# Finishing of output blocks moved and split differently, and the first visit's masks reordered, in a one-core masked graph attention

## The chip, the cores and the metric

The kernel runs on one core of one Trainium2 chip. The metric is the device time of one execution in microseconds (us), lower is better. Five engines work side by side, each through its own instructions in order: TensorE (PE; PEld are its weight loads), VectorE (DVE), ScalarE (ACT), GpSimd (POOL) and the sync engine (SP), which here only issues transfers. They wait for each other by counting semaphores.

## What is computed

```python
h = maximum(layernorm(x), 0)                      # x is 8192 x 256, float32
e = leaky_relu(h @ a[:256] + (h @ a[256:]).T, 0.01)   # 8192 x 8192
att = softmax(where(adj > 0, e, -9e15), axis=1)   # adj is 8192 x 8192, int32
out = x + att @ h
```

A row of adj without any edge gets the mean of h as its result (the softmax of equal values). The kernel calls this the row's share of the mean.

## The kernel before

**Weights.** The exponential of the leaky relu splits into factors of the row and of the column, so a tile of weights is `max(r, g) * mask`, with r laid out along the rows of a block (`r_rep`), g one number per column, and q, the third factor, folded into h. VectorE makes it (`weights`, L766), from the mask turned so that columns lie on partitions (`T8`). For float32 accuracy the weights are split into a rounded part `w_hi`, which ScalarE makes (`round_w`, L534 and L537), and the rest `w_lo`, which VectorE makes (`subtract`, L777 and L781). h times q is split in the same way into `h_hi` (ScalarE) and `h_lo` (GpSimd: `scale_h` L372, `rest_h` L389, L391). TensorE adds three products per tile: hi by hi, lo by hi, hi by lo (`row_tile`, L929 to L932).

**Blocks and visits.** The output has 16 row blocks of 512 rows; columns come in 16 chunks of 512. A chunk is two pairs of 128-column tiles; a pair is 24 products on TensorE. A visit keeps one block's sums in PSUM (`acc`) over some chunks. The first 24 visits do a quarter of the columns (4 chunks, 8 pairs) each; their sums are kept in DRAM (`part_sums`). Then come 8 turns of `finals(m)`, each with a *short visit* (block m, the last quarter, 8 pairs) and a *long visit* (block m+8, all 16 chunks, 32 pairs).

**The mask.** Per chunk ScalarE turns adj into a mask (`convert`, L524, 2 us). Until about 600 us TensorE turns it (L896); in the last visits VectorE does (L747, once per chunk).

**Slots.** Every engine walks through the pairs with the same `steps`. Extra work is hung on slot k of a visit by `side_work(V, k)`: k is 0 to 3 in a visit's first step, 4 to 7 in its second, and 8 to 11 in the last step of a long visit. In slot k VectorE makes `w_lo` of pair k-2, then side work, then the weights of pair k. TensorE may start pair k when `w_hi` and `w_lo` of pair k are there; `w_lo` has two buffers, so VectorE is at most two pairs ahead.

**Finishing.** A block that is complete is finished during the next visit. ScalarE copies the sums out of PSUM into `stage` (`evacuate`, slot 1). In a long visit the block is one whose first three quarters lie in DRAM: ScalarE issues the load of them (`load_prior`, slot 0) and GpSimd adds them (`add_prior`, L400, four instructions). VectorE then makes the reciprocal row sums and the flags of empty rows (`denominators`, L794 to L800, slot 3 in a short visit and slot 4 in a long one). For each of four row tiles ScalarE scales the sums (L591) and makes the share of the mean (`hshare`, L592), and GpSimd adds both to x in `xb` (`finish`, L409 and L411). There is one `hshare`, so ScalarE waits for GpSimd's last add before it goes on:

```python
act.wait_ge(s_o, i)      # in normalise(f, t)
```

x of the block is loaded again in slot 2 (`load_x_again`), and the result is stored from the ScalarE queue in slot 7 of a short and slot 8 of a long visit (`store_out`).

**The first visit** (`head`) makes h for chunks 0 to 3 while it uses it. For each chunk VectorE also makes the scores of the next one (`scores`, L734, eight instructions with their reads) and layer norm statistics (`stats`, L708, L714). TensorE turns the mask of the next chunk behind a chunk's first (even) pair.

## Time and profile before

| what | value |
|---|---|
| time, median of 3 runs | 1568.66 us (1568.29 to 1571.74) |
| the profiled execution: its own time | 1571.44 us |
| its span, first to last instruction | 1569.7 us |
| busy: TensorE, VectorE, ScalarE, GpSimd | 1526.8, 1498.5, 1187.6, 384.0 us |
| mean granted TensorE clock | 0.998 |

The profiled execution took 1.74 us more than its span and lies 2.78 us above the median of the three runs. Busy time is a count of the time in which an engine ran an instruction; it says nothing of who waited for whom, for which the rows below are read.

### The profile page before, as it was taken

To read this page: it belongs to the slowest core of one execution; us is meant where nothing else is said; L and a number is where in the kernel's file an instruction comes from. 1 tells how busy PE (TensorE), PEld (TensorE's weight loads), DVE (VectorE), ACT (ScalarE), POOL (GpSimd) and SP (SyncE) were. 2 spreads that over 40 slices of the span, in tenths; PEclk is the share of its full clock that TensorE was granted. 3 is DMA by queue.
4 is the path that set the end of the run, shared out by engine and by line. 5 is a ranking of instruction groups with operands and counts; after the bars stand their busy time and mean duration, and the time that the engine had idled before them with its cause. 6 is when DMAs were issued, how large, how long until landed. Compare 5 with 4: busy or idle time off the path is not lost.

```text
span 1569.7 us, 39126 instructions
## 1 busy us (share of the span) xinstructions
PE 1526.8 (97%) x12678; PEld 1513.0 (96%) x12678; DVE 1498.5 (95%) x2172; ACT 1187.6 (76%) x1240; POOL 384.0 (24%) x487
## 2 busy tenths in 40 slices
PE   5999999999999999999999999999999999999999
PEld 5899999999999999999999999999999999999998
DVE  7899999999999999999999999999999999999998
ACT  7788887778777777777877877877877877777774
POOL 6263334325453240300310300300300300300400
PEclk9999999999999999999999999999999999999999
DMA  6666677787777799999999999999999999999994
GB/s 206 210 208 227 202 224 222 231 251 226 238 229 236 236 225 226 220 195 207 221 194 204 218 196 203 224 193 207 217 192 206 219 194 205 218 191 209 209 196 100
DMA packets 436488, 330.99 MB, mean 211 GB/s; under 512 B 16704, under 2 KB 378176, under 8 KB 436416
## 3 DMA queue, kind: packets, MB, share of 16 engines
q1 hardware_dynamic: 411360, 288.94, 82.8%
q10 hardware_dynamic: 25056, 41.13, 8.6%
q8 instruction: 41, 0.67, 0.2%
q14 instruction: 31, 0.25, 0.1%
HBM read 308.90 MB, written 21.10 MB: 210 GB/s over the span
## 4 chain that ended last, share of the span: by engine, by line
PE 74%; DMA 8%; DVE 5%; issue 3%; ACT 3%; POOL 2%; SPq 1%; ACTq 0%; DVEq 0%; POOLq 0%
PE acc L929 24%; PE acc L932 24%; PE acc L931 24%; DMA adj_in<-in_adj_dram 6%; PE T L896 2%; DVE w_lo L777 2%; DMA xo<-part_sums 2%; ACT mask L524 2%; DVE halves L766 2%; SPq L265 1%; POOL stage L400 1%; ACT w_hi L534 1%; DVE T L747 1%; POOL xb L409 0%; POOL xb L411 0%
## 5 line engine op out<-in xcount | busy, mean ns | idle before, releaser
L929 PE MATMUL acc<-h_hi,w_hi 128*128 128x258 f32 (+1 forms) x4096 | 1168.6, 285 | 25.2 <-DVE w_lo L777 13.0
L932 PE MATMUL acc<-h_hi,w_lo 128*128 128x258 f32 (+1 forms) x4096 | 1153.3, 282 | 0.0
L931 PE MATMUL acc<-h_lo,w_hi 128*128 128x256 f32 (+1 forms) x4096 | 1149.7, 281 | 0.0
L929 PEld LDWEIGHTS acc<-h_hi,w_hi 128*128 128x128 f32 x4096 | 771.8, 188 | 37.7 <-issue 25.1
L931 PEld LDWEIGHTS acc<-h_lo,w_hi 128*128 128x128 f32 x4096 | 778.5, 190 | 0.1
L932 PEld LDWEIGHTS acc<-h_hi,w_lo 128*128 128x128 f32 x4096 | 775.3, 189 | 0.0
L766 DVE SCALAR_TENSOR_TENSOR halves<-r_rep,g_all,T 128x512 f32<-128x512 f32 (+1 forms) x1024 | 712.9, 736 | 13.6 <-PE T L896 1.9
L524 ACT ACTIVATE mask<-adj_in,mhalf 128x2048 fp8e5<-128x2048 int32 x256 | 510.1, 1993 | 44.0 <-DMA adj_in<-in_adj_dram 39.1
L534 ACT ACTIVATE w_hi<-halves 128x1024 fp32r<-128x1024 f32 x336 | 353.3, 1058 | 175.7 <-DVE halves L766 168.5
L777 DVE SCALAR_TENSOR_TENSOR w_lo<-halves,w_hi 128x1024 fp32r<-128x1024 f32 x336 | 424.5, 1263 | 11.3 <-PE acc L932 5.3
L537 ACT ACTIVATE w_hi<-halves 128x1024 fp32r<-128x1024 f32 x176 | 185.3, 1057 | 101.9 <-DVE halves L766 96.9
L781 DVE SCALAR_TENSOR_TENSOR w_lo<-halves,w_hi 128x1024 fp32r<-128x1024 f32 x176 | 230.8, 1311 | 17.7 <-PE acc L932 8.7
L409 POOL TENSOR_TENSOR xb<-xb,stage 128x256 f32<-128x256 f32 x60 | 48.7, 812 | 644.1 <-ACT halves L592 644.1
L400 POOL TENSOR_TENSOR stage<-stage,xo 128x258 f32<-128x258 f32 x96 | 95.4, 1025 | 215.0 <-DMA xo<-part_sums 137.2
L747 DVE STREAM_TRANSPOSE T<-mask 128x512 f32<-128x512 f32 x168 | 120.7, 718 | 6.0 <-ACT mask L524 6.0
L372 POOL TENSOR_SCALAR halves<-halves,q 128x256 f32<-128x256 f32 x56 | 37.6, 691 | 202.9 <-ACT q L480 172.3
L556 ACT ACTIVATE stage<-acc 128x258 f32<-128x258 f32 x156 | 56.0, 383 | 24.5 <-PE acc L932 23.8
L896 PE MATMUL T<-ident,mask 128*128 128x128 f32 x352 | 53.4, 274 | 13.9 <-ACT mask L524 13.9
L389 POOL TENSOR_TENSOR h_lo<-halves,h_hi 128x256 f32 (+1 forms) x60 | 56.2, 968 | 4.6 <-ACT h_hi L499 4.4
L896 PEld LDWEIGHTS T<-ident,mask 128*128 128x128 f32 x352 | 41.2, 141 | 13.9 <-issue 13.9
L380 POOL TENSOR_TENSOR hsum<-hsum,halves 128x256 f32<-128x256 f32 x48 | 50.7, 1055 | 2.8
L411 POOL TENSOR_TENSOR xb<-xb,halves 128x256 f32<-128x256 f32 x60 | 49.7, 829 | 4.7
(70 smaller groups left out, 316.5 us busy)
## 6 DMA issues: line engine op xcount, KB each, us to landing
adj_in<-in_adj_dram SPq DMA_DIRECT2D x672, 256.0 KB, 5.0
adj_in<-in_adj_dram SPq DMA_DIRECT2D x88, 1024.0 KB, 6.3
part_sums<-stage ACTq DMA_DIRECT2D x24, 516.0 KB, 5.8
xo<-part_sums ACTq DMA_DIRECT2D x24, 516.0 KB, 4.2
r_rep<-r_rows SPq DMA_DIRECT2D x39, 256.0 KB, 4.5
xb<-in_x_dram ACTq DMA_DIRECT2D x15, 512.0 KB, 6.5
out_dram<-xb ACTq DMA_DIRECT2D x15, 512.0 KB, 4.7
xb<-in_x_dram SPq DMA_DIRECT2D x14, 512.0 KB, 6.3
```

The lines of the kernel that those rows point to most:

```text
L400: last = nc.gpsimd.tensor_tensor(stage[:, t, :], stage[:, t, :], prior[:, t, :], ALU.add)
L524: nc.scalar.activation(mask8[:, kc, :, :].rearrange("p t j -> p (t j)"), adj_in[:, kc, :, :].rearrange("p t j -> p (t j)"), ACT.Sign, bias ...
L534: nc.scalar.activation(w_hi[:, k % HL, :].rearrange("p (u j) -> p u j", u=2), deep_w[k], ACT.Relu).then_inc(s_hi, 1)
L537: nc.scalar.activation(w_hi[:, k % HL, :], W[:, k % 2, :], ACT.Relu).then_inc(s_hi, 1)
L747: nc.vector.transpose(T[:, kc, t * P:], mask_words[:, kc, t:G, :]).then_inc(s_TV, 1)
L766: last = nc.vector.scalar_tensor_tensor(out, r_rep[:, V.v % 2, :], g_all[:, ds(G * c + e, 1)], T8[:, k // 2, e, :], ALU.max, ALU.mult)
L777: nc.vector.scalar_tensor_tensor(w_lo[:, k % LL, :].rearrange("p (u j) -> p u j", u=2), deep_w[k], 0.0, w_hi[:, k % HL, :].bitcast(f32).re ...
L781: nc.vector.scalar_tensor_tensor(w_lo[:, k % LL, :], W[:, k % 2, :], 0.0, w_hi[:, k % HL, :].bitcast(f32), ALU.max, ALU.subtract).then_inc ...
L896: last = nc.tensor.transpose(T[:, kc, t * P:(t + 1) * P], mask_words[:, kc, t, :], ident[:])
L929: nc.tensor.matmul(acc[:, t, 0:WC], w_hi[:, k % HL, cols], rhs_hi, start=start and u == 0, stop=False)
L931: nc.tensor.matmul(acc[:, t, 0:D], w_hi[:, k % HL, cols], rhs_lo, start=False, stop=False)
L932: last = nc.tensor.matmul(acc[:, t, 0:WC], w_lo[:, k % LL, cols], rhs_hi, start=False, stop=stop and u == 1)
```

## The change

In four places, with names of the code after it:

1. *Finishing in a long visit.* Denominators go from slot 4 to 5, the reload of x from 2 to 3, the four tiles of `normalise` from slots 4 to 7 to slots 6 to 9, so the last two fall into the visit's last step, and the store from slot 8 to 10. GpSimd's `finish` stands in the last step. The store of the block finished in a short visit goes from that visit's slot 7 to slot 0 of the long visit behind it, behind the issue of `load_prior`.
2. *The share of the mean* (60 times) is made by GpSimd, between its two adds, in place of ScalarE. ScalarE's wait for `s_o` is gone from `normalise`, and a wait on it is added in front of `denominators`.
3. *First visit.* The mask of the next chunk is turned in front of the even pair for chunks 1 to 3; `h_hi` and `h_lo` are signalled in halves in these chunks, so that the even pair waits for two tiles of `h_lo` and not four. `first_round_h` and `first_rest_h`, which served chunk 0 alone, become `early_round_h` and `early_rest_h` for chunks 0 to 3.
4. *Start.* adj of chunk 0 is loaded ahead of x of chunk 1; VectorE makes the scores of chunk 0 ahead of the statistics of chunk 1; ScalarE copies `r_rep` and rounds h of chunk 0 ahead of h of chunk 1.

```diff
@@ load order, sync queue @@
                     load_x(0, 0, False)
                     sp.dma_start(r_rep[:, 1, :], a_row.partition_broadcast(P)).then_inc(s_a, 16)
-                    load_x(1, 1, False)
...
                     if V.head and first and kc == 1:
+                        load_x(1, 1, False)
                         sp.dma_start(x_ahead, x_w[2]).then_inc(s_xa, 16)
@@ GpSimd, chunks 0 to 3 (before: first_rest_h for chunk 0, rest_h for 1 to 3) @@
+            def early_rest_h(m):
+
+                parity = m % CI
+                tiles = slice(G * m, G * (m + 1))
+                pool.wait_ge(s_hq, m + 1)
+                pool.wait_ge(s_h0, G * m + 1)
+                nc.gpsimd.tensor_tensor(h_hi[:, tiles, D + 1:WC], q4[:, parity, :].rearrange("p (e o) -> p e o", o=1),
+                                        h_hi[:, tiles, D:D + 1].bitcast(f32), ALU.subtract)
                 for e in range(G):
+                    tile = slice(G * m + e, G * m + e + 1)
                     if e < G - 1:
-                        pool.wait_ge(s_h0, e + 2)
+                        pool.wait_ge(s_h0, G * m + e + 2)
                     else:
-                        pool.wait_ge(s_hh, 1)
-                    nc.gpsimd.tensor_tensor(h_lo[:, e:e + 1, 0:D], hq[:, e:e + 1, :], h_hi[:, e:e + 1, 0:D].bitcast(f32),
-                                            ALU.subtract).then_inc(s_hl if e == G - 1 else s_l0, 1)
+                        pool.wait_ge(s_hh, m + 1)
+                    done = nc.gpsimd.tensor_tensor(h_lo[:, tile, 0:D], hq[:, e:e + 1, :],
+                                                   h_hi[:, tile, 0:D].bitcast(f32), ALU.subtract)
+                    if e == 1:
+                        done.then_inc(s_l0, 1)
+                    if e == G - 1:
+                        done.then_inc(s_hl, 1)
@@ GpSimd, finish(f, t) @@
                 nc.gpsimd.tensor_tensor(xb[:, t, :], xb[:, t, :], stage[:, t, 0:D], ALU.add).then_inc(s_fin, 1)
+                if not isinstance(i, int) or i > 0:
+                    pool.wait_ge(s_o, i)
+                pool.sem_inc(s_pgate, 1)
+                nc.gpsimd.tensor_scalar(hshare, hmean, zrow[:, t:t + 1], 1.0, ALU.mult, ALU.mult).then_inc(s_share, 1)
                 pool.wait_ge(s_fin, i + 1)
+                pool.wait_ge(s_share, i + 1)
                 nc.gpsimd.tensor_tensor(xb[:, t, :], xb[:, t, :], hshare, ALU.add).then_inc(s_o, 1)
...
-                if V.prev in ("full", "rest") and second:
+                if V.prev == "full" and second or V.prev == "rest" and last:
                     for t in range(G):
                         finish(V.f, t)
@@ ScalarE, exps @@
-                nc.scalar.activation(r_all[:, k], h12[:, parity, 0, :], ACT.Exp, bias=nn[:], scale=1.0 - SLOPE)
+                first_r = nc.scalar.activation(r_all[:, k], h12[:, parity, 0, :], ACT.Exp, bias=nn[:], scale=1.0 - SLOPE)
+                if isinstance(c, int) and c == 0:
+                    first_r.then_inc(s_er, 1)
@@ ScalarE, chunks 0 to 3 @@
-            def first_round_h(tiles):
+            def early_round_h(m, tiles):
...
                 for e in tiles:
-                    nc.scalar.activation(h_hi[:, e:e + 1, 0:D], hb[:, e:e + 1, :], ACT.Copy,
-                                         scale=q4[:, 0, e:e + 1]).then_inc(s_hh if e == G - 1 else s_h0, 1)
+                    nc.scalar.activation(h_hi[:, G * m + e:G * m + e + 1, 0:D], h_bufs[parity][:, e:e + 1, :], ACT.Copy,
+                                         scale=q4[:, parity, e:e + 1]).then_inc(s_hh if e == G - 1 else s_h0, 1)
@@ ScalarE, finishing @@
             def normalise(f, t):
 
-                i = G * f + t
                 if t == 0:
                     act.wait_ge(s_rinv, f + 1)
-                if not isinstance(f, int) or i > 0:
-                    act.wait_ge(s_o, i)
-                nc.scalar.activation(stage[:, t, 0:D], stage[:, t, 0:D], ACT.Copy, scale=rinv[:, t:t + 1])
-                nc.scalar.activation(hshare, hmean, ACT.Copy, scale=zrow[:, t:t + 1]).then_inc(s_y, 1)
+                nc.scalar.activation(stage[:, t, 0:D], stage[:, t, 0:D], ACT.Copy, scale=rinv[:, t:t + 1]).then_inc(s_y, 1)
@@ ScalarE, begin @@
                 exps(0, 0)
-                h_rows(1, 1, [0, 1])
                 act.wait_ge(s_lay, 1)
                 nc.scalar.activation(r_rep[:, 0, :], r_first, ACT.Copy).then_inc(s_r0, 1)
-                first_round_h([0, 1])
+                early_round_h(0, [0, 1])
+                h_rows(1, 1, [0, 1])
@@ ScalarE, side_work @@
-                if V.prev in ("full", "rest") and k == 2:
-                    load_x_again(V)
                 if V.prev == "full":
+                    if k == 2:
+                        load_x_again(V)
                     if 3 <= k < 3 + G:
                         normalise(V.f, k - 3)
-                    if k == 7:
-                        store_out(V)
                 if V.prev == "rest":
-                    if 4 <= k < 4 + G:
-                        normalise(V.f, k - 4)
-                    if k == 2 * PI:
-                        store_out(V)
+                    if k == 0 and not (isinstance(V.f, int) and V.f == 0):
+                        store_out(V.f - 1, V.pb + SH - 1)
+                    if k == 3:
+                        load_x_again(V)
+                    if 6 <= k < 6 + G:
+                        normalise(V.f, k - 6)
+                    if k == 6 + G:
+                        store_out(V.f, V.pb)
@@ VectorE @@
-            stats(1, 1, 1, range(G))
             dve.wait_ge(s_aps, 1)
             scores(0, 0, range(G))
+            stats(1, 1, 1, range(G))
             stats(2, 0, 2, range(G))
...
-                if (V.prev, k) in (("full", 3), ("rest", 4)):
+                if (V.prev, k) in (("full", 3), ("rest", 5)):
                     denominators(V)
@@ TensorE, steps @@
-                    if V.head and m == 0 and k == 0:
-                        pe.wait_ge(s_l0, 2)
+                    if V.head and k % 2 == 0:
+                        if m > 0:
+                            transpose_mask((m + 1) // CI, (m + 1) % CI, True, 0)
+                        pe.wait_ge(s_l0, m + 1)
                     elif V.head:
                         pe.wait_ge(s_hl, m + 1)
...
                     products(V, c + kc, n * PI + k, k, first and k == 0, last and k == PI - 1)
-                    if k % 2 == 0 and V.head:
-                        transpose_mask((m + 1) // CI, (m + 1) % CI, m > 0, 0)
-                    elif k % 2 == 0 and not (V.tail and last):
+                    if V.head and m == 0 and k == 0:
+                        transpose_mask(0, 1, False, 0)
+                    if k % 2 == 0 and not V.head and not (V.tail and last):
                         transpose_mask(n + 1, kc, True, V.dt_next if last else V.dt)
```

TensorE in the first visit, at the start of chunk 1's first pair (`hs_ps` is the sum of h over the rows; L929 to L932 are the products). Before:

```order
L912 MATMUL hs_ps<-stage,one 128x256 [waits normed_tiles]
L912 MATMUL hs_ps<-stage,one 128x256 x3
L929 MATMUL acc<-h_hi,w_hi 128x258 [waits lo_ready,hi_ready,h_lo_ready]
L931 MATMUL acc<-h_lo,w_hi 128x256
L932 MATMUL acc<-h_hi,w_lo 128x258
```

After, same place (the products are L945 to L948, the turning of the mask is L912):

```order
L928 MATMUL hs_ps<-stage,one 128x256 [waits normed_tiles]
L928 MATMUL hs_ps<-stage,one 128x256 x3
L912 MATMUL T<-ident,mask 128x128 [waits w_ready,mask_ready]
L912 MATMUL T<-ident,mask 128x128 x3
L945 MATMUL acc<-h_hi,w_hi 128x258 [waits lo_ready,hi_ready,early_h_lo_half]
L947 MATMUL acc<-h_lo,w_hi 128x256
L948 MATMUL acc<-h_hi,w_lo 128x258
```

The turning of the next mask, with its waits for ScalarE's mask and for the weights, now stands ahead of the pair's 24 products; before, it stood behind them.

VectorE in a long visit, slots 4 and 5 (L747 and L762 turn the mask, `fin` holds the denominators). Before:

```order
L747 STREAM_TRANSPOSE T<-mask 128x512 [waits mask_ready]
L777 SCALAR_TENSOR_TENSOR w_lo<-halves,w_hi 128x1024 [waits pair_used,hi_ready]
L794 TENSOR_TENSOR fin<-stage 128x4 [waits prior_part_added]
L796 TENSOR_SCALAR fin<-fin 128x4 [waits den_step]
L798 TENSOR_TENSOR fin<-fin 128x4 [waits den_step]
L800 RECIPROCAL fin<-fin 128x4 [waits den_step]
L766 SCALAR_TENSOR_TENSOR halves<-r_rep,g_all,T 128x512 [waits lo_ready,mask_transposed_by_vector]
L766 SCALAR_TENSOR_TENSOR halves<-r_rep,g_all,T 128x512
L777 SCALAR_TENSOR_TENSOR w_lo<-halves,w_hi 128x1024 [waits pair_used,hi_ready]
```

After:

```order
L762 STREAM_TRANSPOSE T<-mask 128x512 [waits mask_ready]
L792 SCALAR_TENSOR_TENSOR w_lo<-halves,w_hi 128x1024 [waits pair_used,hi_ready]
L781 SCALAR_TENSOR_TENSOR halves<-r_rep,g_all,T 128x512 [waits lo_ready,mask_transposed_by_vector]
L781 SCALAR_TENSOR_TENSOR halves<-r_rep,g_all,T 128x512
L792 SCALAR_TENSOR_TENSOR w_lo<-halves,w_hi 128x1024 [waits pair_used,hi_ready]
L810 TENSOR_TENSOR fin<-stage 128x4 [waits prior_part_added]
L812 TENSOR_SCALAR fin<-fin 128x4 [waits den_step]
L814 TENSOR_TENSOR fin<-fin 128x4 [waits den_step]
L816 RECIPROCAL fin<-fin 128x4 [waits den_step]
L781 SCALAR_TENSOR_TENSOR halves<-r_rep,g_all,T 128x512 [waits lo_ready,mask_transposed_by_vector]
```

The four small instructions, with their wait for GpSimd's added prior sums, moved behind the weights of slot 4 and the `w_lo` behind them.

GpSimd, the finishing of the first tile and the start of the second (`xb` is x and then the result). Before:

```order
L409 TENSOR_TENSOR xb<-xb,stage 128x256 [waits rows_normalised,x_rows_of_block_loaded]
L411 TENSOR_TENSOR xb<-xb,halves 128x256 [waits finish_step]
L409 TENSOR_TENSOR xb<-xb,stage 128x256 [waits rows_normalised]
L411 TENSOR_TENSOR xb<-xb,halves 128x256 [waits finish_step]
```

After:

```order
L418 TENSOR_TENSOR xb<-xb,stage 128x256 [waits rows_normalised,x_rows_of_block_loaded]
L422 TENSOR_SCALAR halves<-halves,fin 128x256
L425 TENSOR_TENSOR xb<-xb,halves 128x256 [waits share_of_empty_rows_ready,rows_added]
L418 TENSOR_TENSOR xb<-xb,stage 128x256 [waits rows_normalised]
L422 TENSOR_SCALAR halves<-halves,fin 128x256 [waits out_ready]
L425 TENSOR_TENSOR xb<-xb,halves 128x256 [waits share_of_empty_rows_ready,rows_added]
```

Each tile has one more instruction between the two adds, which reads and writes `halves`.

## Rows read from the trace of the kernel before

**Rows 1.** Stretches: PE, PEld, DVE, ACT, POOL busy (instructions), clock, DMA share, GB/s.
```profile
22.00:25.30 3.30, 3.30 (x18) 3.30 (x17) 2.61 (x10) 3.30 (x8) 2.38 (x7) 0.50 0.77 201
25.40:40.00 14.60, 12.88 (x96) 11.98 (x95) 13.31 (x41) 12.03 (x24) 10.69 (x19) 1.00 0.45 147
200.00:400.00 200.00, 200.00 (x1694) 200.00 (x1693) 187.89 (x296) 154.68 (x178) 75.51 (x92) 1.00 0.75 229
1030.00:1085.00 55.00, 55.00 (x466) 55.00 (x465) 54.24 (x69) 40.06 (x30) 0.00 (x0) 1.00 1.01 203
```

**Rows 2.** What TensorE waited for from 620 us on; then from 985 to 1000 us.
```profile
PE acc L929 <- DVE w_lo L777: 12.7, 28, 1.1
PE acc L929 <- ACT w_hi L534: 4.3, 5, 1.3
...
PE acc L929 <- DVE w_lo L777: 0.5, 2, 0.3
```

**Rows 3.** Timeline of TensorE: start, us, instruction, [idle before, releaser].
```profile
1011.19 0.36 PE L929 MATMUL acc<-h_hi,w_hi 128*128 128x258 f32 x1 [0.80 <-ACT w_hi L534]
...
1014.74 0.36 PE L929 MATMUL acc<-h_hi,w_hi 128*128 128x258 f32 x1 [0.46 <-DVE w_lo L777]
```

**Rows 4.** Timeline of VectorE, 1005 to 1014 us.
```profile
1005.57 1.43 DVE L777 SCALAR_TENSOR_TENSOR w_lo<-halves,w_hi 128x1024 fp32r<-128x1024 f32 x1
1007.74 0.17 DVE L794 TENSOR_TENSOR fin<-stage 128x4 f32<-128x4 f32 x1 [0.73 <-POOL stage L400]
...
1008.51 1.41 DVE L766 SCALAR_TENSOR_TENSOR halves<-r_rep,g_all,T 128x512 f32<-128x512 f32 x2
1009.83 1.22 DVE L777 SCALAR_TENSOR_TENSOR w_lo<-halves,w_hi 128x1024 fp32r<-128x1024 f32 x1
...
1012.91 1.69 DVE L777 SCALAR_TENSOR_TENSOR w_lo<-halves,w_hi 128x1024 fp32r<-128x1024 f32 x1
```

**Rows 5.** Timeline of GpSimd, same stretch.
```profile
1003.76 3.84 POOL L400 TENSOR_TENSOR stage<-stage,xo 128x258 f32<-128x258 f32 x4 [9.10 <-DMA xo<-part_sums]
...
1012.77 0.74 POOL L411 TENSOR_TENSOR xb<-xb,halves 128x256 f32<-128x256 f32 x1
```

**Rows 6.** What VectorE and ScalarE waited for from 640 us on.
```profile
DVE fin L794 <- POOL stage L400: 7.1, 8, 1.4
DVE T L747 <- ACT mask L524: 3.9, 6, 0.9
...
ACT mask L524 <- DMA adj_in<-in_adj_dram: 26.3, 23, 3.0
ACT stage L591 <- POOL xb L411: 15.9, 11, 1.8
```

**Rows 7.** Timeline of VectorE, two turned masks a chunk apart.
```profile
1029.73 0.72 DVE L747 STREAM_TRANSPOSE T<-mask 128x512 f32<-128x512 f32 x1
...
1035.23 0.72 DVE L747 STREAM_TRANSPOSE T<-mask 128x512 f32<-128x512 f32 x1
```

**Rows 8.** The page: groups, count, busy us, mean ns, idle before.
```profile
L929 PE MATMUL acc<-h_hi,w_hi 128*128 128x258 f32 (+1 forms) x4096 | 1168.6, 285 | 25.2 <-DVE w_lo L777 13.0
L372 POOL TENSOR_SCALAR halves<-halves,q 128x256 f32<-128x256 f32 x56 | 37.6, 691 | 202.9 <-ACT q L480 172.3
```

**Rows 9.** Timeline of the first visit, VectorE, then ScalarE, then TensorE.
```profile
16.53 0.75 DVE L766 SCALAR_TENSOR_TENSOR halves<-r_rep,g_all,T 128x512 f32<-128x512 f32 x1 [1.07 <-ACT r_rep L609]
...
45.56 0.75 DVE L766 SCALAR_TENSOR_TENSOR halves<-r_rep,g_all,T 128x512 f32<-128x512 f32 x1 [1.33 <-issue]
...
53.80 0.75 DVE L766 SCALAR_TENSOR_TENSOR halves<-r_rep,g_all,T 128x512 f32<-128x512 f32 x1 [0.81 <-PE T L896]
...
39.65 1.99 ACT L524 ACTIVATE mask<-adj_in,mhalf 128x2048 fp8e5<-128x2048 int32 x1
...
41.91 0.39 PE L929 MATMUL acc<-h_hi,w_hi 128*128 128x258 f32 x1 [1.39 <-POOL h_hi L391]
...
58.68 0.36 PE L929 MATMUL acc<-h_hi,w_hi 128*128 128x258 f32 x1 [1.69 <-ACT stage L556]
```

More of the change, by code:

```diff
@@ L163, in masked_graph_attention @@
         s_rinv = sem("rinv_ready")
-        s_fin = sem("finish_step")
+        s_fin = sem("rows_added")
+        s_share = sem("share_of_empty_rows_ready")
         s_y = sem("rows_normalised")
@@ L178, in masked_graph_attention @@
         s_hl = sem("h_lo_ready")
-        s_h0 = sem("first_h_hi_tiles")
-        s_l0 = sem("first_h_lo_tiles")
+        s_h0 = sem("early_h_hi_parts")
+        s_l0 = sem("early_h_lo_half")
+        s_er = sem("first_r_ready")
         s_ns = sem("nshift_ready")
@@ L418, in steps @@
                     scale_h(0, 0)
-                    first_rest_h()
+                    early_rest_h(0)
                     norm(2, 0)
                     scale_h(1, 1)
-                    rest_h(1, 1)
+                    early_rest_h(1)
                     norm(3, 1)
@@ L615, in head_chunk @@
                 if m == 0:
-                    first_round_h([2, 3])
+                    early_round_h(0, [2, 3])
                     store_r(0)
@@ L625, in head_chunk @@
                         h_rows(m + 2, m % CI, [0, 1])
-                    round_h(m + 1, (m + 1) % CI, range(G))
+                    early_round_h(m + 1, range(G))
                     store_r(m + 1)
```

27 lines of the change are left out of this document (12 added, 15 removed).

## The prediction

> **What bounds the kernel now.** I read the stretches first. From 200 to 400 us TensorE is busy in all of 200 us, VectorE in 188 [rows 1]: nothing that another engine does there is worth time, and the change leaves that part alone. The same holds for the quiet part of a long visit, 1030 to 1085 us. What can be won is where TensorE waits. From 620 us on it waited 12.7 + 4.3 = 17.0 us, 33 times [rows 2]. I asked the same view visit by visit: each of the seven short visits with a finishing has 0.3 to 0.5 us of it (one is shown), 3.0 together, so the eight long visits have 14.0, 1.1 to 2.5 each, all in their first third.
>
> Why there: VectorE's chunk takes 1035.23 - 1029.73 = 5.50 us when nothing is added [rows 7], TensorE's 48 products 48 x 55/466 = 5.67 us [rows 1]. VectorE wins back only 0.17 us a chunk, so each addition of more than its small lead shows on TensorE. In the long visit at 1001 us it goes like this. VectorE ends a `w_lo` at 1005.57 + 1.43 = 1007.00, stands 0.73 us until GpSimd has added the prior sums, and spends 1008.51 - 1007.74 = 0.77 on the denominators, all ahead of the weights of slot 4 and the `w_lo` of pair 3 (1009.83 + 1.22 = 1011.05) [rows 4]. GpSimd's adds end at 1003.76 + 3.84 = 1007.60 [rows 5], so that wait is real. TensorE, free since 1010.39, starts pair 3 at 1011.19. The view names `w_hi` as the releaser; by the order of the code it is this `w_lo`, which ended 0.14 us before. Pair 4 waits 0.46 more, behind a `w_lo` of 1.69 us [rows 3, 4]. Every second long visit has a third wait four pairs later: ScalarE stands in `normalise` for GpSimd's last add (15.9 us in all, 11 times), the next mask gets late, and VectorE waits for it (3.9 us in all, 6 times) [rows 6].
>
> In the first visit VectorE sets the pace (busy 13.31 of 14.60 us, TensorE with gaps) [rows 1], and three of its waits are 1.07, 1.33 and 0.81 us, each at the first weights of a chunk [rows 9]. For the second and third the turned mask was late, because TensorE turned it only behind the even pair. The second is called issue in the row; the turning by TensorE ended just before it.
>
> **The change, part by part.**
>
> *Denominators one slot later (8 times).* Followed in the visit at 1001 us: weights of slot 4 from 1007.00 to 1008.32 (1009.83 - 1008.51 = 1.32), `w_lo` of pair 3 to 1009.5, before TensorE is free at 1010.39. The wait of 0.80 is gone. Denominators to 1010.3, weights of slot 5 to 1011.6, the turned mask 0.6, `w_lo` of pair 4 at 1013.4. Pair 4 is due at 1010.39 + 24 x 55/466 = 1013.2. So 0.2 us stay of 0.46. The prior sums have until 1009.5 instead of 1007.0, which covers the 7.1 us of waits for them [rows 6].
>
> *Normalise in slots 6 to 9, without the wait for GpSimd.* ScalarE is not held any more, and the third wait goes with it. Two tiles are left in the first third and two go to the last step, where VectorE is ahead and can lose time unseen. What stays: a `w_lo` that starts while GpSimd runs an add takes up to 1.69 - 1.22 = 0.47 us more [rows 4, 5]. For the two early tiles I take 0.25 us on TensorE. Masks that come late from DRAM (26.3 us of ScalarE waits [rows 6]) stay late: the reload of x and the store move, their bytes do not shrink. I take another 0.25 a visit. Together that is 0.2 + 0.25 + 0.25 = 0.7 us of waits per long visit, 5.6 for 14.0: **-8.4**. About twelve waits fewer also spare the slower first product behind a wait (0.36 us [rows 3]; the mean one has 0.285 [rows 8]): **-0.9**. Bounds for this part: only the wait for GpSimd goes and the rest comes back, -3.2; nearly all goes, -12.4.
>
> *The share on GpSimd (60 times).* GpSimd gets a TENSOR_SCALAR of this shape, 0.69 us in the nearest row [rows 8], 60 x 0.69 = 41 us; it is idle in the quiet part [rows 1] and hides it. ScalarE loses about 0.5 us per tile, off the path. The second add moves back by some 0.3 us. Whether it meets a `w_lo` more or less often I cannot tell: **0** for the short visits, -3 to +3. A rule that speaks against this piece stands in the Trainium skill, SBUF — State Buffer, Who interferes with whom: a VectorE instruction with two SBUF inputs and a GpSimd instruction that reads SBUF take turns on a port, whole instruction by whole instruction. The row of 1.69 us agrees with it. By the rule the new instruction holds the port too; this would give the slower rival below.
>
> *The extra waits.* `denominators` now waits for the last add of the block before, which lies several pairs back in either visit: 0. Behind it on VectorE stand the weights, so if it did bind it would cost as before.
>
> *The store from slot 7 to slot 0 of the next visit.* It is queued on ScalarE behind the issue of the prior load, which reaches its queue first. The reload of x in slot 3 waits for this store, three pairs or 8.5 us behind its issue. 0 where it lands in that time; if not, ScalarE stands there, and the next mask, `w_hi` and TensorE behind it.
>
> *First visit.* With masks turned ahead, the waits of 1.33 and 0.81 go, since VectorE sets the pace and TensorE has gaps for the four short instructions: -2.1. The price is that TensorE waits for ScalarE's mask ahead of an even pair. In chunk 2 this mask ends at 39.65 + 1.99 = 41.64, and the pair started at 41.91 [rows 9], so the pair may lose 0.2 at the old pace, which the next pair gives back, having no turning in front. At the start VectorE does the scores of chunk 0 ahead of the statistics of chunk 1, ScalarE the copy of r sooner; VectorE is then the one that is late, and of the wait of 1.07 I count 0.3 as won. ScalarE's evacuation, which held TensorE until 58.68, stands behind weights of VectorE and moves with them. **-2.4**, between +1.5 and -3.2 (1.33 + 0.81 + 1.07). One more unknown: from 22.0 to 25.3 us the granted clock was 0.50, the lower level of 1.2 GHz, right after TensorE had begun its first pair behind an idle time [rows 1]; if the start moves, this stretch meets other products, at most 1 us either way.
>
> **Sum.** -8.4 - 0.9 + 0 - 2.4 = -11.7 us. The profiled execution took 1571.44 us, so 1559.7 by it; it lies 2.8 above the median of the runs, 1568.66, and from that comes **1557.0 us**.
>
> **Rivals.**
> 1. *The waits move instead of going.* VectorE's deficit and the late masks are the same, so pair 4, 6 or 8 waits for what pair 3 no longer waits. For it: the DMA share of 1.01 even in the quiet part [rows 1]. Against: part of the deficit is pure standing (0.73 of it). Left are about 0.4 per long visit: -3.2 - 2.4 = -5.6, 1563.1 us. Chance 0.22.
> 2. *More goes.* The second add now mostly starts behind the start of a `w_lo`, and a `w_lo` that starts first keeps its 1.22 us. Then the short visits' 3.0 and all but 0.2 per long visit go, with the first products: -12.4 - 3.0 - 1.5 - 2.4 = -19.3, 1549.4 us. Chance 0.10.
> 3. *The mask in front costs the first visit* 1.5 in place of -2.4: 1560.9 us. For it: ScalarE is busy 12.03 of 14.60 us there [rows 1]. Chance 0.07.
> 4. *Slower, by the third GpSimd instruction.* If it holds up a `w_lo` by the full 0.47 each time: 16 tiles lie in last steps with room, 44 x 0.47 = 20.7, less 11.7: +9.0, 1577.7 us. It decides from 11.7/44 = 0.27 us a tile. Against: a `w_lo` starts once in 2.8 us, and the new one fills a time in which the port was free. Chance 0.05.
> 5. My forecast: chance 0.56, by its own 1552.5 to 1561.5 us (long visits -6 to -11, first visit -1 to -3.2, short visits 1 either way).
>
> **Numbers.** About 0.2%, 3.1 us, is what a measurement of this kernel can tell from no change. Faster by more: all of 2, 3 and 5 but a little, and most of rival 1, 0.89. Within: 0.06. Slower: rival 4, 0.05. The range that leaves out rival 4, the better half of rival 2 and the tail of rival 1 is 1551 to 1566 us.
>
> **What the profile after should show.** TensorE's waits from 620 us on near 8 to 9 us in place of 17.0; no wait before the first denominator instruction, none of ScalarE's `normalise` for GpSimd; no TensorE wait at a long visit's pair 3, a small one at pair 4; VectorE's two waits at 45 and 53 us gone, and the first product of the second visit at about 56.3 in place of 58.68. Wrong would be: waits for masks of VectorE above 3.9 us, a mean `w_lo` above the old one in the last visits, or ScalarE standing in slot 3 for the store.

## The result and the profile after

The changed kernel takes 1552.76 us (median of 4 runs, 1550.19 to 1556.14), the kernel before 1568.47 on the same chip (1567.79 to 1571.74): a ratio of 0.9901, interval 0.9878 to 0.9924. On another chip it was 1554.00 (6 runs), again 0.9901 (0.9883 to 0.9920). The profiled execution took 1553.15 us, its span is 1551.3; that of before took 1571.44.

Where the 18.3 us between the two profiled executions went is read from the start of each visit's first product in TensorE's timeline. A long visit is counted to the first pair behind it (the last one to its own last pair).

| stage | before | after | change | predicted |
|---|---|---|---|---|
| start of visit 2 | 58.68 | 54.48 | -4.2 | -2.4 |
| visits 2 to 24 | 567.03 | 566.50 | -0.5 | 0 |
| 8 short visits | 189.88 | 184.85 | -5.0 | 0 |
| 8 long visits | 747.30 | 738.73 | -8.6 | -9.3 |

These are one execution each, and parts of them move from one execution to the next: a second one of the changed kernel (after_again below) has 55.41, 567.15, 186.31 and 735.19 in the four rows.

What TensorE waited for from 620 us on (us in all, times, longest), against [rows 2], and VectorE and ScalarE from 640 us on, against [rows 6]; TensorE waited for no `w_hi`, VectorE not for the prior sums, ScalarE never in `normalise`:

```profile
PE acc L945 <- DVE w_lo L792: 7.0, 12, 2.0
...
DVE T L762 <- ACT mask L541: 5.0, 4, 2.1
...
ACT mask L541 <- DMA adj_in<-in_adj_dram: 42.6, 35, 4.1
```

TensorE's 17.0 us of waits in 33 places became 7.0 in 12. The two other kinds of wait grew: ScalarE waited 42.6 us for adj in place of 26.3, VectorE 5.0 us for masks in place of 3.9.

One short visit as a stretch (us, then PE, PEld, DVE, ACT, POOL busy, clock, DMA share, GB/s). Before:

```profile
977.97:1001.71 23.74, 23.29 (x195) 22.93 (x194) 23.43 (x32) 20.38 (x24) 5.72 (x8) 1.00 1.01 219
```

and after:

```profile
969.18:992.08 22.90, 22.90 (x194) 22.86 (x193) 22.80 (x34) 18.88 (x20) 11.69 (x12) 1.00 1.05 215
```

The same visit is 0.84 us shorter and TensorE is busy in all of it. The timelines of VectorE and GpSimd inside it show what changed. Before (start, us, instruction):

```profile
984.43 1.65 DVE L777 SCALAR_TENSOR_TENSOR w_lo<-halves,w_hi 128x1024 fp32r<-128x1024 f32 x1
...
984.26 0.74 POOL L411 TENSOR_TENSOR xb<-xb,halves 128x256 f32<-128x256 f32 x1
```

After:

```profile
975.97 1.21 DVE L792 SCALAR_TENSOR_TENSOR w_lo<-halves,w_hi 128x1024 fp32r<-128x1024 f32 x1
...
979.05 1.20 DVE L792 SCALAR_TENSOR_TENSOR w_lo<-halves,w_hi 128x1024 fp32r<-128x1024 f32 x1
...
975.33 0.48 POOL L422 TENSOR_SCALAR halves<-halves,fin 128x256 f32<-128x256 f32 x1
975.96 1.82 POOL L425 TENSOR_TENSOR xb<-xb,halves 128x256 f32<-128x256 f32 x1 [0.15 <-POOL halves L422]
...
979.07 1.78 POOL L425 TENSOR_TENSOR xb<-xb,halves 128x256 f32<-128x256 f32 x1 [0.15 <-POOL halves L422]
```

Before, GpSimd's second add is under way when `w_lo` starts, and `w_lo` takes 1.65 us; two later ones in this visit, at 987.95 and 994.08, take 1.68. After, the share (0.48 us) stands between the adds, the add starts with `w_lo`, and now it is the add that takes 1.82 us while `w_lo` keeps 1.21. The `w_lo` of this visit all took 1.20 or 1.21. So in these rows the one that starts second pays, and the order of the starts says who: 1.21 + 0.74 = 1.95 us of work took 1.82 from the first start to the last end, before (984.26 to 986.08) as after (975.96 to 977.78). The Trainium skill, SBUF — State Buffer, Who interferes with whom, has the two take turns on a port and lets the order of issue decide who waits; the rows agree to within 0.13 us.

The first visit, TensorE, the rows that answer to [rows 9] (L912 turns a mask):

```profile
20.32 0.36 PE L945 MATMUL acc<-h_hi,w_hi 128*128 128x258 f32 x1 [2.22 <-DVE w_lo L796]
...
30.78 0.66 PE L912 MATMUL T<-ident,mask 128*128 128x128 f32 x4 [1.79 <-ACT mask L541]
...
39.96 0.66 PE L912 MATMUL T<-ident,mask 128*128 128x128 f32 x4 [1.15 <-ACT mask L541]
...
54.48 0.37 PE L945 MATMUL acc<-h_hi,w_hi 128*128 128x258 f32 x1
```

It now waits for ScalarE's masks of chunks 2 and 3 (the price named in rival 3), but the waits of 1.39 for `h_lo` at 41.91 and of 1.69 for ScalarE's evacuation at 58.68 are gone. The same stretch as in [rows 1] stands at the full clock:

```profile
22.00:25.30 3.30, 2.98 (x25) 2.77 (x25) 3.30 (x10) 2.63 (x8) 3.22 (x5) 1.00 0.86 250
```

Last, the worst place that is left, in the long visit that starts at 1337.15: ScalarE, VectorE, TensorE.

```profile
1351.93 2.00 ACT L541 ACTIVATE mask<-adj_in,mhalf 128x2048 fp8e5<-128x2048 int32 x1 [4.05 <-DMA adj_in<-in_adj_dram]
...
1354.10 0.73 DVE L762 STREAM_TRANSPOSE T<-mask 128x512 f32<-128x512 f32 x1 [2.11 <-ACT mask L541]
...
1356.38 0.36 PE L945 MATMUL acc<-h_hi,w_hi 128*128 128x258 f32 x1 [2.01 <-DVE w_lo L792]
```

A mask that is 4.05 us late costs VectorE 2.11 and TensorE, at pair 6, 2.01.

### The profile page after: what moved, and what is told of

It is laid out like the page before. It is cut to its first block, busy times and chain, and to the rows that moved or that the text cites. A ratio compares the mean times of both kernels' runs of the same rounds, so it can differ in the third digit from the quotient of the medians.

```text
span 1551.3 us, 39208 instructions
## 1 busy us (share of the span) xinstructions
PE 1521.7 (98%) x12678; PEld 1511.9 (97%) x12678; DVE 1495.6 (96%) x2172; ACT 1163.1 (75%) x1180; POOL 446.4 (29%) x547
## 4 chain that ended last, share of the span: by engine, by line
PE 83%; DMA 5%; DVE 3%; issue 2%; ACT 2%; SPq 1%; ACTq 0%; DVEq 0%
PE acc L945 27%; PE acc L948 27%; PE acc L947 27%; DMA adj_in<-in_adj_dram 5%; PE T L912 2%; ACT mask L541 1%; DVE w_lo L792 1%; SPq L267 1%; DVE halves L781 1%; ACT w_hi L551 1%; DVE T L762 0%; DVE w_lo L796 0%; ACT w_hi L554 0%; DVE adj_in L896 0%; DVE adj_in L891 0%
## 5 line engine op out<-in xcount | busy, mean ns | idle before, releaser
L945 PE MATMUL acc<-h_hi,w_hi 128*128 128x258 f32 (+1 forms) x4096 | 1167.2, 285 | 10.3 <-DVE w_lo L792 7.0
L948 PE MATMUL acc<-h_hi,w_lo 128*128 128x258 f32 (+1 forms) x4096 | 1153.3, 282 | 0.0
L945 PEld LDWEIGHTS acc<-h_hi,w_hi 128*128 128x128 f32 x4096 | 772.0, 188 | 17.8 <-issue 7.4
L948 PEld LDWEIGHTS acc<-h_hi,w_lo 128*128 128x128 f32 x4096 | 775.4, 189 | 0.0
L418 POOL TENSOR_TENSOR xb<-xb,stage 128x256 f32<-128x256 f32 x60 | 59.3, 988 | 646.5 <-ACT stage L605 612.0
L409 POOL TENSOR_TENSOR stage<-stage,xo 128x258 f32<-128x258 f32 x96 | 99.0, 1063 | 192.1 <-DMA xo<-part_sums 115.8
L762 DVE STREAM_TRANSPOSE T<-mask 128x512 f32<-128x512 f32 x168 | 120.5, 717 | 6.3 <-ACT mask L541 6.1
L912 PE MATMUL T<-ident,mask 128*128 128x128 f32 x352 | 53.5, 274 | 15.7 <-ACT mask L541 15.7
L425 POOL TENSOR_TENSOR xb<-xb,halves 128x256 f32<-128x256 f32 x60 | 61.5, 1025 | 9.1 <-POOL halves L422 7.4
L912 PEld LDWEIGHTS T<-ident,mask 128*128 128x128 f32 x352 | 41.0, 141 | 16.6 <-issue 12.7
L389 POOL TENSOR_TENSOR hsum<-hsum,halves 128x256 f32<-128x256 f32 x48 | 47.1, 982 | 2.8
L398 POOL TENSOR_TENSOR h_lo<-halves,h_hi 128x256 f32 (+1 forms) x48 | 45.7, 982 | 3.5 <-ACT h_hi L515 3.5
```

Of the source, the lines that this page charges most:

```text
L409: last = nc.gpsimd.tensor_tensor(stage[:, t, :], stage[:, t, :], prior[:, t, :], ALU.add)
L762: nc.vector.transpose(T[:, kc, t * P:], mask_words[:, kc, t:G, :]).then_inc(s_TV, 1)
L912: last = nc.tensor.transpose(T[:, kc, t * P:(t + 1) * P], mask_words[:, kc, t, :], ident[:])
L945: nc.tensor.matmul(acc[:, t, 0:WC], w_hi[:, k % HL, cols], rhs_hi, start=start and u == 0, stop=False)
L948: last = nc.tensor.matmul(acc[:, t, 0:WC], w_lo[:, k % LL, cols], rhs_hi, start=False, stop=stop and u == 1)
```

## The experiments

Times are medians; ratios are to the kernel before, timed on the same chip (1568.91, 1568.42 and 1569.84 us in the three sets). "Undone" means that the lines of the diff above are as before.

### One part undone at a time

**share_back**: ScalarE makes the share again and waits for GpSimd; the late slots stay.

```diff
-                nc.gpsimd.tensor_scalar(hshare, hmean, zrow[:, t:t + 1], 1.0, ALU.mult, ALU.mult).then_inc(s_share, 1)
...
+                    act.wait_ge(s_o, i)
...
+                nc.scalar.activation(hshare, hmean, ACT.Copy, scale=zrow[:, t:t + 1]).then_inc(s_y, 1)
```

> The changed kernel with the share of the mean made by ScalarE again (its wait for GpSimd's last add too, and the extra wait before the denominators gone). Theory: in the short visits GpSimd's second add used to run when a w_lo was about to start and held it up; the share between the two adds moved it behind the start of a w_lo. So each short visit gets its two waits of TensorE back, 0.8 us each and 5 us in seven, w_lo of 1.6 us appear there again, and the long visits lose 1 to 3 us, because ScalarE is held again: 1552.8 + 7 = 1560 us. Rival: ScalarE's shorter work made the gain; then the time is about the same, but the w_lo of the short visits stay near 1.21 us and the waits are for w_hi. A second rival, that this part is worth nothing and all came with the later finishing: 1553 us.

Measured 1573.64 us, ratio 1.0034 (1.0017 to 1.0050): all of the gain is gone, and more. The profiled execution took 1569.15. Its waits from 620 us on:

```profile
ACT stage L603 <- POOL xb L420: 22.5, 20, 3.1
PE acc L943 <- DVE w_lo L791: 19.0, 22, 2.4
DVE T L761 <- ACT mask L536: 18.2, 20, 2.5
```

I had expected most of the loss in the short visits, with `w_lo` of 1.6 us back in them. It is in the long ones. The seven short visits that finish a block took 162.4 us here, 160.8 in the changed kernel and 166.1 in the kernel before; the eight long visits took 751.2, 738.7 and 747.3. The chain in a long visit is seen at pair 8: ScalarE stands 1.05 to 1.31 us for GpSimd's add, VectorE 0.60 for the mask, TensorE 0.40 to 0.64, in seven of the eight. TensorE's larger wait is at pair 6, 10.9 us over the eight visits (5.5 in the changed kernel). It follows ScalarE's waits for adj in slot 4, 25.3 us here and 17.8 there, and these stand ahead of any wait for GpSimd in that visit. How holding ScalarE makes adj come later is not shown by a row of its own.

In the short visit at 978 us a wait for GpSimd is seen by itself:

```profile
989.57 0.51 ACT L603 ACTIVATE stage<-stage,fin 128x256 f32<-128x256 f32 x1 [1.49 <-POOL xb L420]
```

The add was long because it met a `w_lo` that had started first. That visit took 22.8 us, so the 1.49 us cost TensorE nothing there. The mean `w_lo` here is 1235 ns, below the 1263 of before, so held-up `w_lo` are not what made this kernel slow. They are short in the short visits too, though ScalarE makes the share: x landed 5.6 to 8.9 us after the start of these visits, in the kernel before 4.7 to 5.2, and GpSimd's first add waited for it and so came later.

**finish_back**: the slots of denominators, reload, `normalise` and store undone; the rest stays.

```diff
-                if (V.prev, k) in (("full", 3), ("rest", 5)):
+                if (V.prev, k) in (("full", 3), ("rest", 4)):
...
-                    if 6 <= k < 6 + G:
-                        normalise(V.f, k - 6)
+                    if 4 <= k < 4 + G:
+                        normalise(V.f, k - 4)
```

> The changed kernel with the finishing in the slots of before (denominators slot 4, reload of x slot 2, normalise 4 to 7, stores in slot 7 and 8). Theory: the wait before the denominators comes back (7 us in 8 long visits) and with it TensorE's wait at pair 3 of each long visit, 0.6 to 1.3 us; the waits by ScalarE for GpSimd stay away. 1552.8 + 7 = 1560 us, the short visits unchanged. Rival: the waits only move within the long visit because masks come late from DRAM, so the later slots are worth 0 to 2 us: 1553 to 1555 us.

Measured 1556.24 us, ratio 0.9926 (0.9903 to 0.9948): only 3.5 us above the changed kernel, with overlapping intervals. From 620 us on:

```profile
PE acc L943 <- DVE w_lo L790: 7.2, 14, 1.2
DVE fin L808 <- POOL stage L409: 6.8, 8, 1.3
```

The wait for the prior sums is back with its old size, and TensorE's waits are still 7.2 us. By pairs of the eight long visits (the time from one pair's start to the next above 2.85 us), the wait ahead of pair 3 is 6.1 us here and 0.1 in the changed kernel, but the one ahead of pair 6 is 2.1 here and 5.5 there. My largest term, the later slots, won what it was to win at pair 3 and lost part of it at pair 6. How much is not sure: after_again has 3.8 there and two_shares, with the same slots, 1.4.

**mask_back**: the mask is turned behind the even pair again, the halves of `h_lo` stay.

```diff
-                        if m > 0:
-                            transpose_mask((m + 1) // CI, (m + 1) % CI, True, 0)
                         pe.wait_ge(s_l0, m + 1)
...
+                    if V.head and k % 2 == 0:
+                        transpose_mask((m + 1) // CI, (m + 1) % CI, m > 0, 0)
```

> The changed kernel with the next mask turned behind the even pair again in the first visit. Theory: VectorE's waits of 1.33 and 0.81 us for the turned mask come back, and the second visit starts 2.1 us later than in the changed kernel: 1555 us. Rival: TensorE's own wait for ScalarE's mask in front of a pair ate the gain, and the second visit starts within 0.5 us of 54.5: 1553 us.

Measured 1554.64 us, ratio 0.9919 (0.9894 to 0.9944), 1.9 above the changed kernel, within the intervals. TensorE in the first visit has its old last wait again:

```profile
56.53 0.36 PE L945 MATMUL acc<-h_hi,w_hi 128*128 128x258 f32 x1 [1.69 <-ACT stage L573]
```

From the first pair to visit 2 it takes 36.29 us; the kernel before took 37.83, and eight of the nine other experiments that turn the mask in front took 35.3 to 35.4 (the ninth, share_two_buffers, stood longer at the lower clock and took 36.47). So the mask in front is worth 1.0 us and the halves of `h_lo` 1.5. VectorE's waits for the turned mask say the same. Of its two of before, 1.33 at 45.56 and 0.81 at 53.80 [rows 9], only the second is back:

```profile
51.65 1.41 DVE L781 SCALAR_TENSOR_TENSOR halves<-r_rep,g_all,T 128x512 f32<-128x512 f32 x2 [0.92 <-PE T L912]
```

The 1.33 stays away with the mask behind the pair, so it was the late pair, which waited 1.39 us for `h_lo`, that had made that mask late.

**start_back**: the start undone (x of chunk 1 loaded ahead of adj, the old orders on ScalarE and VectorE).

```diff
+                    load_x(1, 1, False)
...
+            stats(1, 1, 1, range(G))
             dve.wait_ge(s_aps, 1)
             scores(0, 0, range(G))
-            stats(1, 1, 1, range(G))
```

> The changed kernel with the start of before: x of chunk 1 ahead of adj, statistics of chunk 1 ahead of the scores of chunk 0, h of chunk 1 ahead of r. Theory: the first pair starts 0.5 us later, as in the kernel before, and that is all that this part gave: 1553.3 us. Rival: the start also decided that the granted clock did not fall behind the first pair (0.50 for 3.3 us before, 1.00 after); then the stretch at 0.50 is back and the second visit starts 1.5 to 2 us later: 1555 us.

Measured 1551.06 us, ratio 0.9889 (0.9865 to 0.9913). The first pair began at 19.87 us, in the changed kernel at 20.32. The start is worth nothing that can be measured.

### What the share on GpSimd does

**gap_in_before**: the kernel before, with an instruction of the share's shape between GpSimd's two adds; its result is not used. ScalarE still makes the share and still waits.

```diff
                 nc.gpsimd.tensor_tensor(xb[:, t, :], xb[:, t, :], stage[:, t, 0:D], ALU.add).then_inc(s_fin, 1)
-                pool.wait_ge(s_fin, i + 1)
+                nc.gpsimd.tensor_scalar(hsum[:], hmean, zrow[:, t:t + 1], 1.0, ALU.mult, ALU.mult).then_inc(s_fin, 1)
+                pool.wait_ge(s_fin, 2 * i + 2)
```

> The kernel before with one idle GpSimd instruction of the share's kind between the two adds of each tile (its result is used by nobody); everything else, ScalarE's share and its wait too, as before. Theory: the order in which the second add and a w_lo start decides who waits; 0.5 us later the second add starts behind the w_lo, so the 1.65 us w_lo of slots 4 and 6 of the short visits become 1.21 and the short visits lose their 0.8 us each (166.1 to about 161 us for seven), although GpSimd does more and ScalarE is held longer. The long visits get no better, or 1 to 5 us worse, since ScalarE waits for GpSimd. Rival: ScalarE's shorter work made the short visits' gain; then seven of them still take 166 us or more.

Measured 1580.56 us, ratio 1.0077 (1.0052 to 1.0102). The total missed what I expected, and so did the seven short visits, 169.4 us and not 161. TensorE's wait at their pair 4 did go, from 3.0 us over the seven to nothing, since the second add now starts with the `w_lo`. But GpSimd is longer by its new instruction, and ScalarE hangs on it:

```profile
ACT stage L592 <- POOL xb L412: 39.1, 24, 2.2
...
ACT mask L525 <- POOL xb L412: 13.7, 7, 2.0
DVE T L748 <- ACT mask L525: 13.5, 25, 1.6
```

39.1 us in place of 15.9 [rows 6], and 13.7 more where a mask stands behind the store, which waits for the last add. So the gap alone moves the loss off the first `w_lo` and onto ScalarE, at a price above the gain.

**share_two_buffers**: ScalarE makes the share, but into two buffers in turn, and waits for the add two tiles back.

```diff
+                if not isinstance(f, int) or i > 1:
+                    act.wait_ge(s_o, i - 1)
...
+                nc.scalar.activation(hsum[:] if t % 2 else hshare, hmean, ACT.Copy, scale=zrow[:, t:t + 1]).then_inc(s_y, 1)
```

> The changed kernel with the share made by ScalarE again, but into two buffers in turn, so that ScalarE waits for the add of two tiles before and not for the last one. Theory: what cost 21 us in the run with the share given back was ScalarE held by GpSimd while masks were late, 22.5 us of waits; without most of them the time is within 4 us of the changed kernel, 1553 to 1557 us. Rival: ScalarE's 0.5 us of added work per tile was the cost; then it stays at 1565 us or more.

Measured 1555.28 us, ratio 0.9908 (0.9890 to 0.9926), 18 us below share_back with ScalarE doing the same work. The one row left of the chain:

```profile
ACT stage L603 <- POOL xb L420: 1.7, 1, 1.7
```

It was the wait for the single `hshare` that cost, and not the 0.5 us a tile of ScalarE's work. The rest of the code is the same in the two kernels, and x is late in the short visits of both (5.7 to 9.4 us after their start).

**two_shares**: GpSimd makes the share twice, the first time into a buffer that nobody reads.

```diff
+                nc.gpsimd.tensor_scalar(hsum[:], hmean, zrow[:, t:t + 1], 1.0, ALU.mult, ALU.mult).then_inc(s_share, 1)
                 nc.gpsimd.tensor_scalar(hshare, hmean, zrow[:, t:t + 1], 1.0, ALU.mult, ALU.mult).then_inc(s_share, 1)
```

> The changed kernel with the new GpSimd instruction twice per tile, the first time into a buffer that nobody uses. It doubles the cost that my slower rival named. Theory: the port goes to the instruction that starts first, and what counts is where an add stands against the start of a w_lo; GpSimd's own length costs nothing, so 1552 to 1556 us. Rival (the added instruction holds up VectorE by up to 0.47 us each): 0.2 to 0.4 us more per tile, 12 us and more, 1565 us.

Measured 1552.56 us, ratio 0.9900 (0.9876 to 0.9924). GpSimd's groups (count, busy us, mean ns):

```profile
L422 POOL TENSOR_SCALAR hsum<-halves,fin 128x256 f32<-128x256 f32 x60 | 45.0, 750 | 0.0
L423 POOL TENSOR_SCALAR halves<-halves,fin 128x256 f32<-128x256 f32 x60 | 41.6, 693 | 0.0
```

45 us more of GpSimd cost nothing that can be measured. Rival 4, the slower one, falls, but not because `w_lo` were spared: in the seven short visits 16 of 56 took over 1.4 us (21 in the kernel before, 4 in the changed one), and the visits took 161.0 us, as in the changed kernel. Held up this much, VectorE was still in time for TensorE.

**share_alone**: the kernel before with the share on GpSimd, and nothing else of the change.

```diff
+                nc.gpsimd.tensor_scalar(hshare, hmean, zrow[:, t:t + 1], 1.0, ALU.mult, ALU.mult).then_inc(s_share, 1)
...
-                    act.wait_ge(s_o, i)
...
-                nc.scalar.activation(hshare, hmean, ACT.Copy, scale=zrow[:, t:t + 1]).then_inc(s_y, 1)
```

> The kernel before with one part of the change alone: GpSimd makes the share of the mean, and ScalarE does not wait for its last add. All slots, the first visit and the start are as before. Theory (the release of ScalarE is what the change is worth from 620 us on, and the first visit gives about 3.2 us of its own): the time with the old slots and the new first visit was 1556.2, so here 1556.2 + 3.2 = 1559.4, some 9 us below before. Rival (the parts need each other; without the new first visit and slots the share brings at most the 4 us that ScalarE's turned waits showed in VectorE): 1564 or more.

Measured 1557.75 us, ratio 0.9922 (0.9901 to 0.9943), that is -12 us of the -15.7.

```profile
PE acc L943 <- DVE w_lo L790: 6.3, 9, 2.6
```

This run also says which half of the move helped the short visits. The seven took 159.9 us in place of 166.1, and only 1 of their 56 `w_lo` is over 1.4 us. Yet ScalarE stood for GpSimd in each of them, ahead of the store in slot 7, and longer than before (17.3 us in all; before, 4.4):

```profile
993.15 2.00 ACT L541 ACTIVATE mask<-adj_in,mhalf 128x2048 fp8e5<-128x2048 int32 x1 [2.40 <-POOL xb L425]
```

TensorE is busy in all of the 22.8 us of this visit. So it was the order of add and `w_lo` that helped, and not fewer waits of ScalarE. Its shorter work was not needed either: the visit at 978 us in share_back took 22.8 us as well, with the share still made by ScalarE.

**first_visit_alone**: the change to the first visit and the start; finishing and share undone, as in share_back and finish_back together.

> The change to the first visit and the start alone; finishing and share are those of before. Theory: the second visit starts about 3.2 us sooner (55.4 to 55.5 in place of 58.68) and nothing else moves, so 3 us below before, 1565.2. Rival (what is won in the first visit is lost again later, since the weights are ahead by no more than two pairs and TensorE is full anyway): less than 1 us. If the clock in 22 to 25.3 us is 1.00 and not 0.50, 1 us more is gone.

Measured 1567.10 us, ratio 0.9983 (0.9969 to 0.9996), 2.7 us below before. Visit 2 starts at 55.65. The waits from 620 us on are those of before:

```profile
ACT stage L603 <- POOL xb L420: 14.7, 11, 1.8
PE acc L941 <- DVE w_lo L789: 11.5, 25, 1.6
```

The kernels now stand in a square, all with the new first visit (ratios to before):

| | old slots | new slots |
|---|---|---|
| ScalarE makes the share and waits | 0.9983 (first_visit_alone) | 1.0034 (share_back) |
| GpSimd makes the share | 0.9926 (finish_back) | 0.9901 (the changed kernel) |

The share is worth 0.57% or 9 us in the old slots and 1.33% or 21 us in the new ones. The later slots are a loss of 0.5% without it, and with it a gain of 0.25%, which these runs do not tell from none.

### The late masks

**reload_later**: x is loaded again in slot 5 in place of 3, the tiles go to slots 7 to 10, the store to 11.

```diff
-                    if k == 3:
+                    if k == 5:
                         load_x_again(V)
-                    if 6 <= k < 6 + G:
-                        normalise(V.f, k - 6)
-                    if k == 6 + G:
+                    if 7 <= k < 7 + G:
+                        normalise(V.f, k - 7)
+                    if k == 7 + G:
                         store_out(V.f, V.pb)
```

> The changed kernel with the reload of x in slot 5 of the long visits in place of 3, and normalise in slots 7 to 10, the store in 11. Theory: TensorE's wait at pair 6 (5.5 us in eight visits) is the mask that comes late from DRAM because prior load, store and reload fall together; with the reload two slots later the masks of slots 4 and 6 come in time and 2 to 4 us go: 1550 us. Rival: the wait only moves to pair 8 or 10, since the same bytes are moved with the same small surplus: within 1 us of 1552.8.

Measured 1550.30 us, ratio 0.9869 (0.9847 to 0.9892). From 620 us on:

```profile
PE acc L945 <- DVE w_lo L792: 4.6, 7, 1.5
...
ACT mask L541 <- DMA adj_in<-in_adj_dram: 53.4, 38, 3.7
```

The masks are late by more in all (53.4 us; from 620 us on the changed kernel has 46.3), but not where it hurts: ScalarE's waits for adj in slot 4 of the long visits, the mask that pair 6 needs, fell from 17.8 to 4.5 us, those in slot 6 rose from 3.6 to 11.5, and pair 6 waits 0.3 us in place of 5.5. The tiles moved by one slot too, but they stand behind slot 4 in both kernels, so the waits there answer to the reload. The visit with the worst place of above, 1340 to 1365 us, in the changed kernel:

```profile
1340.00:1365.00 25.00, 22.99 (x181) 22.81 (x180) 22.29 (x31) 16.89 (x15) 8.07 (x9) 0.93 1.16 205
```

and here:

```profile
1340.00:1365.00 25.00, 25.00 (x210) 24.85 (x210) 24.90 (x35) 17.72 (x15) 4.18 (x4) 1.00 1.18 216
```

The DMA engines are as full in both (share 1.16 and 1.18). That the reload stands ahead of adj in their queues is inferred from the slots that changed, and no row shows the queue itself.

**reload_later_old_start** puts start_back on top of it, and **after_again** is the changed kernel, on the same chip.

> The version with the reload of x in slot 5, the tiles in slots 7 to 10 and the store in slot 11, and with the old order of the start. If the start is worth nothing, as its undoing in the changed kernel said, 1550 to 1551; if its undoing is a gain of 1.7 us of its own, 1548.6; if the two lean on each other, 1552 or more.

> The changed kernel again, on the same chip as the three others, so that they are compared with it without a step over two chips. Expected 1552.8 as before; the slots of the version beside it (reload of x in 5) should then be about 2.5 us below it. If they are not, what the earlier run showed was the chip and not the reload.

They took 1550.55 us (ratio 0.9869, 0.9847 to 0.9891) and 1554.00 us (0.9901, 0.9883 to 0.9920). The later reload is about 3.4 us better than the changed kernel here and 2.5 in the other set; the intervals just overlap each time, and both sets point the same way. The waits do so more clearly: ahead of pair 6 both kernels with the later reload have 0.3 us, the two executions of the changed kernel 5.5 and 3.8, with 4.5 and 3.3 us for adj in slot 4 against 17.8 and 19.7. The start is worth nothing with it either.

## Why the prediction came out

The forecast was 1557.0 us and the time 1552.76, at the near edge of the forecast's own range, 1552.5 to 1561.5, and closer to rival 2's 1549.4. Term by term:

- **Later slots and the end of ScalarE's wait, -8.4 and -0.9.** The long visits changed by -8.6 us (-12.1 with the second execution of the changed kernel). The sum holds, its split does not. I had most of it from pair 3, in one visit: that wait is indeed gone (8.0 to 0.1 over eight visits), also most of pair 4's (5.0 to 1.2). But the square shows the later slots alone at +0.5% and the release of ScalarE as what carries them. I had priced the 15.9 us of `normalise` waiting for GpSimd [rows 6] as the third wait of every second long visit; these waits, 1.05 to 1.79 us each, stood in all eight long visits, in three of them twice, and in no short one. That the total came out although the two parts need each other is luck.
- **Rival 1 came in part.** Pair 6 took 3.6 us more than before (1.9 to 5.5), in the second execution 1.9 more. I took "another 0.25 a visit" for late masks, 2 us, so the first is nearly twice that and the second is that. The sign I had named as wrong, VectorE's waits for masks above 3.9 us, did show: 5.0, and 4.6 in the second execution.
- **The share on GpSimd, 0 for the short visits: the term that was mis-sized.** It is -5.0 us, beyond my bound of -3. I had counted only the waits that the view of waits showed there (3.0), and said I could not tell the order of `w_lo` and add. A 0.48 us instruction put the add behind the start of `w_lo`, which is rival 2's mechanism, and TensorE's delays at pairs 4 and 6 of these visits, 0.43 and 0.35 us each, went. ScalarE's release has no part in it that can be seen: in the short visits of the kernel before it stood for GpSimd in `normalise` for 0.02 us at most, and in share_alone it stood for the store longer than before while the visits got shorter. gap_in_before has the order without the release, and the wait at pair 4 went, 3.0 us. share_two_buffers (short visits 185.4 us, 4.5 less than before) is no case of the release without the order, since the late x put the add behind `w_lo` there as well (2 of 56 `w_lo` over 1.4 us).
- **Rival 4** fell with two_shares. The price of **rival 3**, TensorE's waits for masks in the first visit, was paid (1.79 and 1.15 us) and won back.
- **The store in slot 0 of the next visit, 0.** No row has ScalarE standing in slot 3 for it.
- **First visit, -2.4.** From the first pair to visit 2 it is 35.3 to 35.4 us in place of 37.83: -2.5, with -2.7 for first_visit_alone in the medians. The size is right and the reasons are half so. I gave -2.1 to the mask in front, which is worth 1.0; the halves of `h_lo`, to which I gave no term, removed the 1.39 us at 41.91, and with them VectorE's 1.33, and are worth 1.5; the start, to which I gave 0.3, nothing. "The evacuation moves with them" was wrong as well: it got ahead of TensorE and its 1.69 us went. The -4.2 of the table has two more pieces: the first pair happened to be 0.5 sooner, and pair 0 met no stretch at 0.50 of the clock. That is the "1 us either way", here 35.3 less 34.16 = 1.2 us.

The terms off by most, -5.0 and -1.8 against +0.7, and -0.5 in visits 2 to 24, account for the 6.6 us between my 1559.7 for the profiled execution and its 1553.15. In the medians the miss is 4.2 us, since the profiled execution of before lay 2.97 us above its median and that of after 0.39.

What stays open: how ScalarE's waits for GpSimd in the late slots make adj come later and TensorE wait at pair 6, and why x lands later in the short visits of share_back and share_two_buffers.

## What to carry over

When a helper engine hands over one buffer at a time, price the engine that waits for it by all that is queued behind the wait, not by the work that moves: here a second buffer was worth 18 us, and the move of a 0.5 us instruction 21 us in the new slots and 9 in the old. Two moves that look separate can need each other; the later slots lost time until the wait was gone. And where loads are late and DMA is full, moving a burst changes which load is late, so put it where the consumer has slack. An experiment that was to change one thing can change the order of two others: look at the starts in its trace before it is read.

## What the hardware showed that I had not expected

- A shift of 0.2 us in the start of a GpSimd add decides who is held: add first, `w_lo` 1.65 to 1.69 us and add 0.74; `w_lo` first, 1.20 to 1.21 and add 1.78 to 1.82.
- Behind TensorE's idle 2.01 us before 1356.38 the granted clock fell to its lower level of 1.2 GHz: products 0.42 us long in place of 0.28 from 1356.90 to 1359.70. The stretch:

```profile
1356.40:1359.80 3.40, 3.40 (x17) 3.40 (x18) 3.40 (x4) 3.08 (x3) 3.25 (x5) 0.54 1.21 202
```

  A long wait can so cost more than its own length: 17 products here in the time of some 29 (3.40 / 0.118, by the 55 / 466 us of [rows 1]), another 1.4 us. It does not always. Of the four waits of over 2 us in the last visits of all profiled executions, those of 2.01 (here), 2.44 (share_back) and 2.34 us (share_two_buffers) were each followed by such a stretch, and the longest, 2.62 us in share_alone at 638.67, was not.
- The start shows a like stretch in all profiled executions but one: 22.0 to 25.3 us stood at 0.50 to 0.84 of the clock in the others, and at 1.00 in that of the changed kernel, whose TensorE had waited 2.22 us before its first pair as others had 1.88 to 3.25. It is not the kernel that decides this: the second execution of the changed kernel stood at 0.80.
